# One core of a Trainium2 chip: each stage's weights loaded during the stage before it, into three lasting rooms of SBUF

## The reference

```python
x = L0_attn_x
x = _layernorm(x + _L0_attn_ref(x, ...), axis=-1)   # encoder of 6 layers, 16 heads
x = _layernorm(x + _L0_ffn_ref(x, ...), axis=-1)    # shared and 8 routed experts, top 2
x = _layernorm(x + _L1_attn_ref(x, ...), axis=-1)   # gated delta rule, with a rotating scan
x = _layernorm(x + _L1_ffn_ref(x, ...), axis=-1)    # gated network on weights rounded to FP4
x = _layernorm(x + _L2_attn_ref(x, ...), axis=-1)   # linear attention
x = _layernorm(x + _L2_ffn_ref(x, ...), axis=-1)    # network on ternary weights, 128-512-512-512-128
x = _layernorm(x + _L3_attn_ref(x, ...), axis=-1)   # causal attention with rotary positions
x = _layernorm(x + _L3_ffn_ref(x, ...), axis=-1)    # y = real(ifft(fft(x) @ w)) + bias
```

## Time and profile before

| | us |
|---|---|
| median of 3 runs | 4095.8 |
| lowest and highest run | 4094.0, 4099.04 |
| the profiled execution | 4093.98 |
| its span, first to last instruction | 4092.1 |

### The profile page before, as it was taken

How to read it: one execution, slowest core, us unless ns; L and a number is a source line. 1 busy time by engine, 2 the same in 40 slices (tenths; PEclk the granted TensorE clock), 3 DMA queues, 4 the chain that set the end, 5 groups by cost and what they waited for, 6 DMA issues and landing times. The chain is left out here.

```text
span 4092.1 us, 68321 instructions
## 1 busy us (share of the span) xinstructions
PE 3362.9 (82%) x25711; PEld 2345.6 (57%) x25711; DVE 2512.2 (61%) x6468; ACT 1836.8 (45%) x3001; POOL 1057.8 (26%) x1362
## 2 busy tenths in 40 slices
PE   5999999999999999996768586777566659997996
PEld 3666666666666666665668254556354424444674
DVE  4865875775775875874510698886685741115663
ACT  1565565565565565664534552222232213332443
POOL 1324324324324324322454110000201320004321
PEclk8999999999999999998789786998776669997997
DMA  5423534434433534430155100000000000004430
GB/s 134 117 71 98 116 73 99 115 73 100 115 73 97 117 74 99 116 91 1 41 160 181 47 1 0 1 0 1 6 1 5 1 29 0 0 0 110 94 81 26
DMA packets 177020, 262.06 MB, mean 64 GB/s; under 512 B 19950, under 2 KB 149230, under 8 KB 159694
## 3 DMA queue, kind: packets, MB, share of 16 engines
q1 hardware_dynamic: 152494, 140.93, 12.3%
q10 hardware_dynamic: 19656, 107.37, 12.0%
q0 software_dynamic: 4544, 9.38, 0.7%
HBM read 184.67 MB, written 72.19 MB: 63 GB/s over the span
## 5 line engine op out<-in xcount | busy, mean ns | idle before, releaser
L870 DVE TENSOR_REDUCE enc_mx<-psum 128x2 f32<-128x512 f32 (+1 forms) x1152 | 755.6, 685 | 155.7 <-PE psum L550 153.0
L1036 ACT ACTIVATE enc_e<-psum 128x1024 f32<-128x1024 f32 (+1 forms) x768 | 580.3, 808 | 400.4 <-PE psum L571 309.3
L550 PE MATMUL psum<-enc_ks,enc_qs 80*128 80x128 bf16 (+1 forms) x3072 | 459.5, 253 | 69.4 <-DVE enc_mx L870 55.2
L571 PE MATMUL psum<-enc_qs,enc_ks 83*128 83x256 bf16 (+1 forms) x3072 | 380.3, 249 | 29.6 <-DMA enc_qs<-enc_turned_max 21.0
L550 PEld LDWEIGHTS psum<-enc_ks,enc_qs 80*128 80x128 bf16 x3072 | 221.6, 99 | 190.5 <-DVE enc_mx L870 110.4
L584 PE MATMUL psum<-enc_e,enc_v 128*32 128x256 f32 (+1 forms) x6144 | 330.7, 333 | 0.0
L571 PEld LDWEIGHTS psum<-enc_qs,enc_ks 83*128 83x128 bf16 x3072 | 258.2, 98 | 67.8 <-DMA enc_qs<-enc_turned_max 21.4
L584 PEld LDWEIGHTS psum<-enc_e,enc_v 128*32 128x32 f32 x6144 | 160.6, 109 | 161.3 <-ACT enc_e L1036 50.8
L2781 PE MATMUL psum<-ter_h,par_s 128*128 128x512 f32 x512 | 224.9, 593 | 2.4 <-DVE ter_h L2832 1.6
L640 PE MATMUL psum<-par_layerr,enc_hidden 128*128 128x128 f32 x1536 | 191.6, 279 | 16.2 <-DVE enc_n_rows L915 16.2
L640 PEld LDWEIGHTS psum<-par_layerr,enc_hidden 128*128 128x128 f32 x1536 | 182.4, 194 | 26.9 <-DVE enc_n_rows L915 21.2
(11 more groups left out here) (531 smaller groups left out, 7235.3 us busy)
## 6 DMA issues: line engine op xcount, KB each, us to landing
enc_qs<-q_pieces ACTq DMA_DIRECT2D x234, 192.0 KB
enc_ks<-k_pieces ACTq DMA_DIRECT2D x234, 192.0 KB
k_pieces<-enc_pieces SPq DMA_DIRECT2D x240, 128.0 KB, 2.0
moe_wb<-moe_w SPq DMA_DIRECT2D x39, 512.0 KB
q_pieces<-enc_pieces SPq DMA_DIRECT2D x144, 128.0 KB, 2.0
enc_qs<-q_pieces SPq DMA_DIRECT2D x54, 192.0 KB
enc_ks<-k_pieces SPq DMA_DIRECT2D x54, 192.0 KB
rope_qs<-q_pieces ACTq DMA_DIRECT2D x39, 192.0 KB
```

The source lines that it names most:

```text
L550: last = T_.matmul(p1[f % 2][:, i * kw:(i + 1) * kw], qs[0:KEYED, slot, h, j * P:(j + 1) * P], ks[0:KEYED, slot, h, 0:kw], start=True, sto ...
L571: last = T_.matmul(p2[ch][:, g], ks[0:SCORED, slot, 4 * T + g, ch * P:(ch + 1) * P], qs[0:SCORED, slot, 4 * T + g, 0:n], start=True, stop= ...
L870: V.tensor_reduce(mx[:, u % 2, j * HEADS + h0:j * HEADS + h0 + n], p1[f % 2].rearrange("p (h k) -> p h k", h=n), AX_X, ALU.max)\
L1036: A.activation(e_of(T, ch), p2[ch], ACT.Exp, scale=HD ** -0.5).then_inc(s_e, 1)
```

## The change

The loads of s3 to s8 are issued one stage earlier, at the start of the block before, and go into three tiles that outlive the stages: room a (s3, then s5, then s7), room b (s6) and room c (s4, then s8). `encoder` and `experts` keep their own way of loading. No wait is taken out: each stage's engines still wait for their weights, by the same semaphores. The diff, cut to its kinds of edit:

```diff
@@ experts, SP's block @@
             W.start(sp)
+            c.ahead["s3"].start(sp)
             spare = EXPERTS * SLOT_T
             sp.dma_start(x_slots[EXPERTS * REGION:].rearrange("(p r) w -> p (r w)", p=P),
...
@@ delta_rule; the same in fp4_network (s4), linear_attention (s5), ternary_network (s6), rope_attention (s7), fft_mix (s8) @@
-        W = load_stage(c, ctx, "s3")
+        W = c.ahead["s3"]
...
@@ delta_inputs, SP's block; the same in fp4_network (s5), ternary_network (s7), rope_attention (s8) @@
-            W.start(sp)
+            c.ahead["s4"].start(sp)
...
@@ linear_attention, SP's block @@
-            W.start(sp)
+            c.ahead["s6"].start(sp)
             sp.wait_ge(s_cut, 5)
             sp.dma_start(bias3[:], bcut[:].rearrange("p a w -> p (a w)")).then_inc(s_bias, 16)
...
@@ class load_stage @@
-    def __init__(self, c, ctx, name):
+    def __init__(self, c, ctx, name, room=None):
         self.layout, width = c.layouts[name]
-        self.sb = ctx.enter_context(c.nc.sbuf_tensor(f"par_{name}", [P, width], F32))
+        self.sb = room[:, 0:width] if room is not None else ctx.enter_context(c.nc.sbuf_tensor(f"par_{name}", [P, width], F32))
...
@@ build @@
-        for stage in (encoder, experts, delta_rule, fp4_network, linear_attention, ternary_network, rope_attention, fft_mix):
+        c.ahead, rooms = {}, {}
+        stages = ((encoder, None, None), (experts, "s3", "a"), (delta_rule, "s4", "c"), (fp4_network, "s5", "a"), (linear_attention, "s6", "b"),
+                  (ternary_network, "s7", "a"), (rope_attention, "s8", "c"), (fft_mix, None, None))
+        for stage, following, room in stages:
+            if following:
+                if room not in rooms:
+                    rooms[room] = sb("weights_" + room, [P, max(layouts[f][1] for _, f, r in stages if r == room)])
+                c.ahead[following] = load_stage(c, ctx, following, rooms[room])
             base = stage(c, base)
```

More of the change, by code:

```diff
@@ L1166, in sb @@
         def sb(n, shape, dt=F32): return ctx.enter_context(nc.sbuf_tensor("rope_" + n, shape, dt))
-        W = load_stage(c, ctx, "s7")
+        W = c.ahead["s7"]
         scored = PIECES + 3
@@ L1221, in _ @@
         def _(sp):
-            W.start(sp)
+            c.ahead["s8"].start(sp)
             for slot in range(SLOTS):
@@ L1638, in sb @@
         def sb(n, shape, dt=F32): return ctx.enter_context(nc.sbuf_tensor("fft_" + n, shape, dt))
-        W = load_stage(c, ctx, "s8")
+        W = c.ahead["s8"]
         freq_t, mix, y = sb("freq_t", [P, 2, P]), sb("mix", [P, P]), sb("y", [P, 2, GROUP])
@@ L2181, in sb @@
         def sb(n, shape, dt=F32): return ctx.enter_context(nc.sbuf_tensor("fp4_" + n, shape, dt))
-        W = load_stage(c, ctx, "s4")
+        W = c.ahead["s4"]
         HBLOCKS, XBLOCKS, WBLOCKS = TILES * FF4 // BLK, GROUP // BLK, 9 * P // BLK
@@ L2208, in _ @@
         def _(sp):
-            W.start(sp)
+            c.ahead["s5"].start(sp)
         @block.gpsimd
@@ L2413, in sb @@
         def sb(n, shape, dt=F32): return ctx.enter_context(nc.sbuf_tensor("lin_" + n, shape, dt))
-        W = load_stage(c, ctx, "s5")
+        W = c.ahead["s5"]
         KD, PAIR = KVH * HD, KVH * VW * HD
@@ L2736, in sb @@
         def sb(n, shape, dt=F32): return ctx.enter_context(nc.sbuf_tensor("ter_" + n, shape, dt))
-        W = load_stage(c, ctx, "s6")
+        W = c.ahead["s6"]
         silu = sb("silu", [P, 2, GROUP])
@@ L2751, in _ @@
         def _(sp):
-            W.start(sp)
+            c.ahead["s7"].start(sp)
         @block.gpsimd
```

## The result

| | before | after |
|---|---|---|
| median, us (4 runs each) | 4097.42 | 4071.76 |
| lowest and highest run, us | 4094.0, 4099.2 | 4066.18, 4076.63 |
| the profiled execution, us | 4093.98 | 4066.18 |
| its span, us, and granted clock | 4092.1, 0.901 | 4064.3, 0.904 |

The ratio is 0.993, with a 95% interval of 0.9916 to 0.9945: the change makes the kernel faster by 25.7 us by the medians (predicted 27.3). The profiled executions differ by 27.8 us.

What follows compares the result with a forecast made beforehand. Engines standing still for weights at stage starts were taken as the bound. Five starts gain 28.47 us, linear attention loses 1.2: 27.3 less than 4095.8 gives 4068.5 us, range 4060 to 4078.

Steps and rivals of the forecast that it cites:

- The starts: At five stage starts the waiting engine would start with SP's issue, gaining its whole distance, together 28.47 us.
- B: Rival: the five starts hide a stall for a new block's code, 3.1 us each, giving 4084.0 us; chance 0.12.
- The ternary network: PE's start, first in every chain of this stage, would come 9.60 us earlier and shorten the stage by that.
- The delta rule and the FP4 network: Starts of PE and ACT would come earlier, shortening the delta rule by 6.35 us and the FP4 network by 4.36.
- Linear attention: The early start is lost because the small DMA of `lin_bias` waits behind the load of s6: 1.2 us loss.
- C: Rival: in linear attention the small DMA goes past the load of s6, gaining 2.98 us, giving 4064.3; chance 0.14.
- some 0.4 us later: Linear attention: the small DMA lands this much behind the load of s6, itself landing 9.6 us after issue.
- Rope attention: PE's start would gain 4.88 us; POOL's clearing would be done 0.4 us before its first need, costing nothing.
- The last stage: Starting without waiting for weights would make this stage 3.28 us shorter.
- The clock: TensorE's clock at the delta rule, ternary network and rope attention starts: 1.5 us more or less each, taken as zero.
- D: Rival: without its pause the ternary network gets a granted clock of 0.86, 42.7 us more, giving 4111.2; chance 0.03.
- E: Rival: the waits fall on something the rows hide, and the time stays at 4095.8 us; chance 0.03.

Runs made afterwards that it cites:

- after_third: The kernel after, with no edit, run once more in a third group: 4074.11 us against 4106.77 for the kernel before, ratio 0.9925.
- rope_mask_later: The kernel after, with DVE's wait for POOL's clearing and the cast of `rope_neg` moved to the first use of `rope_v`: 4076.61 us, ratio 0.9919.
- bias_ahead_of_s6: The kernel after, with the small DMA of `lin_bias` issued ahead of the load of s6 in linear attention: 4070.3 us, ratio 0.9918.
- all_ahead: The kernel after, with s2 loaded at the encoder's end, `lin_bias` ahead of s6, and rope attention's wait and mask cast later: 4069.39 us, ratio 0.9909.

## Why the prediction was right, point by point

**The starts.** The step was that each waiting engine would start with SP. It held at all five. Four have distances of 0.02 to 0.05 us instead of 4.36 to 9.60; in the last stage, where SP issues nothing now, PE's idle time fell by 3.27 us. B, a stall of some 3.1 us for code, would have shown as a gap of that size ended by a sequencer. The gaps that are left end with the barrier, at the same moment at which SP issues. ACT's 3.94 us before the delta rule, on which B rested, stand there again with the same figure and hold nobody. The Trainium skill, page "Runtime: NRT & Kernel Launch", section "Instruction fetch mechanics", has a stall only where the branch's target isn't fetched yet; the start of a block isn't such a place by these rows.

**The ternary network: 9.60 predicted, 9.6 in every one of the nine profiles.** That is the best-founded part of the result: PE is the first in the chain, it fills the stage, and the stage's length repeats to 0.1 us.

**The delta rule and the FP4 network: right on average, not in the first pair.** Predicted 6.35 and 4.36. The means over the table are 634.9 us (5 profiles with its own load) against 628.2 (8 profiles), 6.7 less, and 225.5 against 219.6, 5.9 less. The first pair of profiles showed 4.0 and 0.5. For the FP4 network the pace explains it; for the delta rule, whose length spreads by 4 us over the five profiles with its own load and by 6 over the eight with it ahead, no cause was sought.

**The experts: nothing predicted, nothing seen above the spread.** In the two faster groups they take 312.9 to 315.9 us with the load of s3 in their queue (after, after_third, rope_mask_later, bias_ahead_of_s6), and 312.5 in the one profile without it. A cost of a microsecond or two isn't excluded.

**Linear attention: the mechanism was right, a term was mis-sized.** The small DMA waited behind the load, and the early start was lost. C is refuted: the projection came at 9.04 us behind the start, and not at 5.85; the kernel with the order reversed had it at 5.83 (5.78 behind PE's first row, which starts 0.05 behind SP), so C's figure was right for that order. The term of "some 0.4 us later" than the load was taken from a transfer of 257 KB. The projection started at 3136.05, and the load landed 9.2 us behind 3127.01, at 3136.21: the small DMA was through no later than the load itself, and the load was 0.4 us faster than the 9.6 assumed. The loss was 0.2 us instead of 1.2, and the stage 0.0 to 0.1 longer. The Trainium skill's rule of order within a ring (page "DMA: Bandwidth & Descriptors", section "Queues, rings and completion order") agrees with the two orders: by it the 1.1 KB wait, on each DMA engine that they use, for that engine's part of the 2824.5 KB ahead of them, and they took 5.14 us there against 1.92 us alone.

**Rope attention: this step failed.** The prediction said that POOL's clearing "is first needed at 3699.92", POOL's own add. DVE needs it earlier: its block has a wait for the clearing (L1523) ahead of its first product. Before, that wait ended with POOL's row at 3694.62, while DVE still waited for weights until 3695.31, so it left no trace:

```profile
3695.31 0.29 DVE L1522 CAST rope_neg<-par_s 128x256 bf16<-128x256 f32 x1 [7.50 <-DMA par_s<-par_in_s]
...
3697.51 0.69 DVE L1497 TENSOR_TENSOR rope_part<-psum,par_s 128x512 f32<-128x512 f32 x1 [1.91 <-PE psum L1323]
```

The clearing takes 4.20 us from the stage's start, and the first product could have come after 2.18. The gain at the first product was 7.06 - 4.23 = 2.83 us and at POOL's add 9.47 - 5.60 = 3.87, instead of 4.88. With the wait moved, the add came at 4.53: 4.94 earlier than before, the predicted gain in full.

At the end of the stage the account is less sure. It is 3.7 us shorter on average: 338.8 over five profiles with its own load, 335.1 over four with the weights there and the wait kept. With the wait moved the mean is 335.7, no shorter. The eight profiles with the weights there fall into 333.8 to 334.5 us with PE busy for 296.2 to 297.5, and 336.9 to 337.7 with PE busy for 299.5 to 301.5, and both kinds occur with and without the wait. So the wait is shown to hold the start, but not to be what is missing of the 4.88 at the end.

The rows couldn't show the wait, the code could: the cover has to be sought on every engine that waits for it, and not just on its own.

**The last stage: 3.28 predicted.** It has two lengths with the weights there, 58.3 to 59.5 us (5 profiles) and 61.5 to 61.6 (3), against 61.7 to 62.7 before. The mean is 2.3 us less. PE starts 3.27 us earlier in any case. What is lost in the three long ones goes with the clock: the window of all_ahead from PE's first row to the end is

```profile
4007.04:4067.61 60.57, 32.02 (x92) 19.46 (x92) 20.41 (x115) 14.94 (x24) 8.31 (x8) 0.53 0.09 35
```

and the kernel after has PE busy for 28.76 us at 0.62 there. The other two long ones have 31.91 and 32.00 at 0.53, the other four short ones 28.98 to 29.79 at 0.56 to 0.62. DVE's and ACT's busy times are equal within 0.2 us. In the first 8 us the clock is 0.50 in the long ones and 0.57 to 0.61 in the short ones. None of the five profiles with its own load is of this kind; whether the shorter pause brings it, three of eight don't tell. The prediction's allowance for the clock had three starts in it, and not this one.

**The clock.** The allowance of 1.5 us at three starts was about right as a spread, and zero as its mean: the ternary network's clock is 0.99 instead of 0.97. Part of this is that the pause at its start is no longer in the window: counted from PE's first row, it was 0.98 before. PE's busy time in it fell by just 0.36 us (313.60 to 313.24). D is refuted.

**The sum.** Means of the stages give 6.7 + 5.9 + 9.6 + 3.7 + 2.3 = 28.2 us, against the 28.47 - 1.2 = 27.3 of the prediction: rope attention and the last stage gave 2.2 less, linear attention 1.2 more, the FP4 network and the delta rule 1.9 more, part of it pace. The 27.8 us of the first pair of profiles agree with it in part by luck: 5.5 of them come from an encoder that nobody touched, and whose 13 profiles reach from 1964.7 to 1978.6 us.

**E** is refuted by every start.

## What to carry to other kernels

Where stages are separated by barriers and begin with a load, the distance from the load's issue to the first row that it releases is what loading ahead gives; but follow the code of each engine for waits that the load hides now, because a wait that is already satisfied leaves no row. A small transfer on which somebody waits belongs ahead of a large one in the same queue, even where it is issued some microseconds later. And a gain of a few microseconds is read from the stage that it falls in, over several profiles: a single pair put 5.5 us into an untouched stage and hid 4 us in a changed one.

## What the runs showed of the hardware

**DVE held up by POOL's clearing.** With weights there at the start, DVE's first rows fall into the time in which POOL clears a tile. In the delta rule DVE's row of L3081 took 0.35 us in the kernel before, when POOL was long done, and 2.32 us in the kernel after (rows above): it ended at 2280.55, just behind POOL's clearing, which ended at 2277.71 + 2.69 = 2280.40. It took 2.31 or 2.32 in every profile with the weights there, and 0.35 in every one without. Nobody waited for it: ACT and PE went on. The cast of `rope_neg`, begun 0.24 us ahead of POOL's clearing of `rope_v`, took 3.90 us in the kernel after and 0.45 us in after_third and the other profiles in which it stands there, where POOL's row was the one that grew:

```profile
3675.97 0.45 DVE L1522 CAST rope_neg<-weights_a 128x256 bf16<-128x256 f32 x1 [2.69 <-PEq L2731]
...
3676.22 3.66 POOL L1293 MEMSET rope_v<- 128x4096 f32 x1
...
3680.28 1.29 DVE L1497 TENSOR_TENSOR rope_part<-psum,weights_a 128x512 f32<-128x512 f32 x2 [3.86 <-POOL rope_v L1295]
```

Against the kernel after, POOL's row is 0.14 us longer (3.66 and 3.52) and DVE's 3.45 us shorter. The Trainium skill, page "SBUF — State Buffer", section "Who interferes with whom", has the two engines share a pair of ports, which the first to issue keeps for its whole instruction when DVE uses both pairs, as a cast or a `tensor_scalar` can. The row of L3081, begun 0.52 us behind POOL's, and the rows of after_third fit that. The long cast does so only in part: its row begins 0.24 us ahead of the clearing of `rope_v` and still ends behind it. POOL's shorter clearing of `rope_cut` (0.31 us) ran just then, in both kernels, and the rows don't tell who was first. Whether a held-up cast would delay the first product, once the wait for the clearing is out of the way, stays open: it was long in one profile only.

**Groups of runs differ by more than the change is worth.** The kernel before took 4097, 4107, 4140 and 4145 us in the four groups. The experts account for most of it: with the same code they took 312.5 us in the first and 348.2 and 349.3 in the groups with 4140 and 4145, and over all kernels 312 to 316 in the faster two and 344 to 357 in the slower two. Each chip was met in one group only, so that it is the chip and not the occasion isn't shown. The change's gain was of the same size in the three groups where it was measured by itself: 25.7, 28.8 and 32.7 us.
